# Token sums of squares: GpSimd takes the sixteenth tile too, TensorE sums one tensor instead of two, one third of a tile later

## The reference

```python
gu = jnp.einsum('bsd,hd->bsh', x, wq_gu)
gate, up = jnp.split(gu, 2, axis=-1)
h = jax.nn.silu(gate) * up
hn = rms_norm(h)            # h * rsqrt(mean(h*h over the 2048 hidden values) + eps)
return jnp.einsum('bsh,dh->bsd', hn, wq_p)
```

## Time and profile before

| | |
|---|---|
| median of three runs | 1183.12 us (1183.0 to 1185.53) |
| the profiled execution, its own time | 1185.58 us |
| its span in the trace | 1184.0 us |
| mean granted TensorE clock | 0.937 |
| TensorE busy | 1077.5 us, 91% |
| VectorE busy | 869.1 us, 73% |
| ScalarE busy | 525.2 us, 44% |
| GpSimd busy | 171.3 us, 14% |
| GpSimd's additions of squares (L2258), 52 | 79.6 us, 1532 ns each |

### The profile page before, as it was taken

How to read it: one execution, slowest core, us unless ns; L and a number is a source line. 1 busy time by engine, 2 the same in 40 slices (tenths; PEclk the granted TensorE clock), 3 DMA queues, 4 the chain that set the end, 5 groups by cost and what they waited for, 6 DMA issues and landing times. The chain is left out here.

```text
span 1184.0 us, 12999 instructions
## 1 busy us (share of the span) xinstructions
PE 1077.5 (91%) x4360; PEld 522.0 (44%) x4360; DVE 869.1 (73%) x1602; ACT 525.2 (44%) x1103; POOL 171.3 (14%) x143
## 2 busy tenths in 40 slices
PE   6788778799979999888998999999998999999997
PEld 2435545444534444334443454444444444444443
DVE  3887776756756778797687899577887677785654
ACT  3655654445525385244263364164444263531421
POOL 3100000211202221030121131122102000100100
PEclk9888765699998999899998999999999999999999
DMA  8511111532400333222130003012010011010000
GB/s 272 180 54 36 54 36 27 187 107 72 126 0 19 118 92 104 69 79 89 56 95 18 27 27 98 16 40 101 27 63 10 1 60 30 18 72 0 1 36 35
DMA packets 47618, 75.53 MB, mean 64 GB/s; under 512 B 8416, under 2 KB 16096, under 8 KB 47424
## 3 DMA queue, kind: packets, MB, share of 16 engines
q1 hardware_dynamic: 47264, 74.62, 19.9%
q0 software_dynamic: 288, 0.09, 0.2%
HBM read 66.16 MB, written 8.54 MB: 63 GB/s over the span
## 5 line engine op out<-in xcount | busy, mean ns | idle before, releaser
L1517 PE MATMUL g_g<-h,wt 128*128 128x512 f16 x1728 | 401.2, 381 | 5.8 <-DVE hid L1824 3.1
L1517 PEld LDWEIGHTS g_g<-h,wt 128*128 128x128 bf16 (+1 forms) x1728 | 168.4, 98 | 223.8 <-issue 35.5
L1531 PE MATMUL g_d<-wt,parts 128*128 128x512 bf16 (+1 forms) x864 | 208.5, 384 | 4.5 <-DVE tmp L1654 2.7
L2144 ACT ACTIVATE parts<-hid 128x512 f16<-128x512 f32 x108 | 68.0, 629 | 303.3 <-DVE hid L1824 303.2
L1439 PE MATMUL g_o<-shared 128*128 128x512 f32 x384 | 183.3, 621 | 14.4 <-DVE tmp L1613 6.4
L1817 DVE SCALAR_TENSOR_TENSOR hid<-th,g_g 128x512 f32<-128x512 f32 x108 | 73.6, 681 | 135.8 <-ACT th L2137 135.7
L1531 PEld LDWEIGHTS g_d<-wt,parts 128*128 128x128 f16 x864 | 84.1, 99 | 114.5 <-issue 16.6
L2258 POOL TENSOR_TENSOR acc<-acc,sqh 128x512 f32<-128x512 f32 x52 | 79.6, 1532 | 297.1 <-ACT sqh L2150 297.1
L1439 PEld LDWEIGHTS g_o<-shared 128*128 128x128 f32 x384 | 75.0, 199 | 98.4 <-issue 72.5
L1829 DVE TENSOR_TENSOR parts<-hid,parts 128x512 f16<-128x512 f32 x108 | 89.6, 830 | 26.0 <-ACT parts L2144 25.9
L2238 POOL TENSOR_TENSOR g_rstd<-g_var,g_power 128x4 f32<-128x4 f32 x20 | 24.2, 1210 | 328.9 <-DVE g_var L1557 328.9
(11 more groups left out here) (329 smaller groups left out, 1511.5 us busy)
## 6 DMA issues: line engine op xcount, KB each, us to landing
shared<-in_w SPq DMA_DIRECT2D x48, 256.0 KB, 2.7
x<-in_codes SPq DMA_DIRECT2D x32, 264.0 KB, 3.1
w_raw<-in_wt SPq DMA_DIRECT2D x16, 512.0 KB, 3.5
x<-in_wmod SPq DMA_DIRECT2D x7, 1024.0 KB, 5.2
wmod<-in_wmod SPq DMA_DIRECT2D x5, 1024.0 KB, 11.5
codes_f<-x SPq DMA_DIRECT2D x32, 132.0 KB, 1.7
gates<-in_x SPq DMA_DIRECT2D x4, 1024.0 KB, 8.2
shared<-in_wt SPq DMA_DIRECT2D x8, 512.0 KB, 4.7
```

The lines of the kernel that those rows point to most:

```text
L1517: mm = nc.tensor.matmul(pg[i][:], wide[:, k, o:o + P], h16[f % 2][:, s, k], start=(s == 0 and k == 0), stop=(s == 1 and k == KD - 1))
L1531: mm = nc.tensor.matmul(pd[j][:], parts16[:, t % 3, s, j * P:(j + 1) * P], wd[:, m, :], start=(m == 0 and s == 0), stop=(done and s == 1))
L2144: nc.scalar.activation(parts16[:, t % 3, 0], hid[:, t % 2], ACT.Copy).then_inc(hi_ready, 1)
```

## The change

GpSimd also adds the square of tile 15, so there are 15 additions per group. TensorE makes the token sums from `acc` alone, with four matmuls per group. The sums, their mean and their root move by one slot: on TensorE from before the group's last product to after it, on VectorE from before `low_part` to after it, right in front of `residual` (in the slot's own order the root comes before the attention steps of that slot). ScalarE's squares of a new group's first two tiles wait for GpSimd's additions, and no longer for TensorE's sums.

```diff
-    ADDS = M0 - 2
+    ADDS = M0 - 1
...
-    SUMS = [3 * M0 * (i + 1) + 1 for i in range(NG)]
+    SUMS = [3 * M0 * (i + 1) + 2 for i in range(NG)]
...
             pe.wait_ge(acc_ready, (f + 1) * ADDS)
-            pe.wait_ge(sq_ready, (f + 1) * M0)
             for j in range(NJ):
-                for i, rows in enumerate((acc, sqh[:, (M0 - 1) % 2])):
-                    mm = nc.tensor.matmul(dst[:, j:j + 1], rows[:, j * P:(j + 1) * P], ones[:, 0:1],
-                                          start=(i == 0), stop=(i == 1))
+                mm = nc.tensor.matmul(dst[:, j:j + 1], acc[:, j * P:(j + 1) * P], ones[:, 0:1], start=True, stop=True)
             mm.then_inc(full, 1)
...
                 elif f:
-                    wait_full(act, "sums", f - 1)
+                    act.wait_ge(acc_ready, f * ADDS - 1 + m)
...
-            if t < NG * M0 and 1 <= t % M0 < M0 - 1:
+            if t < NG * M0 and t % M0:
                 squares(t)
```

## The result

The changed kernel took 1187.15 us in the median of 20 runs (1183.73 to 1190.08), the kernel before 1183.21 us in the median of 20 (1179.17 to 1187.52). The ratio is 1.0028, with a 95% interval of 1.0017 to 1.0038: slower by 2.0 to 4.5 us. The forecast was 1184.7 us with a range of 1181.5 to 1187.0 and "no change" as the likeliest sign. It started from a median of 1183.12 us, and 1183.12 x 1.0028 = 1186.4 us lies inside the range. But it is slower by over 0.2%, and the interval of 2.0 to 4.5 us leaves out the +1.55 us of the forecast's own case.

What follows compares the result with a forecast made beforehand. The bound was taken to change by place: TensorE or a chain of VectorE and ScalarE. Group ends 1 to 4 gave 0.5 - 0.8 - 0.35 + 2.2 = +1.55 us on 1183.12, so 1184.7 us, range 1181.5 to 1187.0.

Steps and rivals of the forecast that it cites:

- the forecast's own case: Whole kernel: the four group ends sum to +1.55 us, giving 1184.7 us; chance 0.42.
- Group 2: End of group 2: VectorE's wait of 0.78 us for the sums goes away, -0.8 us.
- group 4: End of group 4: later root without cover and a low part held up by GpSimd's addition, +2.2 us.
- bare root: End of group 4: nothing hides the root in its new place, so VectorE waits for it, 1.25 us.
- clash: Groups 3 and 4: VectorE's low part must wait for GpSimd's fifteenth addition, about 1.0 us each.
- the end of the first launch: End of group 1: the root ends later than root and product did before, delaying TensorE's restart, +0.5 us.
- Rival 1: Every group end: TensorE is the bound, so all 3.4 us are gained, 1179.7 us; chance 0.12.
- Rivals 3 and 4: Addition holds up nothing at groups 3 and 4, 1183.3 us, chance 0.14; group 4's delay is absorbed, 1182.5 us, chance 0.08.
- group 3: End of group 3: VectorE 0.8 us late, TensorE 0.85 early; spare time at 721.70 and 729.66 leaves -0.35 us.
- TensorE's idle time before 891.46: Behind group 4: grows from 3.16 us to 4 to 5 us with VectorE's delay; otherwise the forecast is wrong.
- TensorE's 0.35 us: Group 4: TensorE gains 0.85 us, its product waits 1.2 us for the low part, leaving it 0.35 us behind.
- Rival 2: Behind group 4, at 891.46: longer TensorE idleness brings a slower clock, 1.6 us on top, 1186.3 us; chance 0.24.

Runs made afterwards that it cites:

- four matmuls alone: Kernel before with four instead of eight sum matmuls per group, leaving out the sixteenth tile's square: 1179.17 us, ratio 0.9959.
- the addition alone: Kernel before with a fifteenth GpSimd addition, eight matmuls kept, so the sixteenth tile's square counts twice: 1183.09 us, ratio 0.9995.
- old slot: Changed kernel with sums and root moved back to their earlier place in all groups: 1182.76 us, ratio 0.9985 against the kernel before.
- group 4 back: Changed kernel with only group 4's sums moved back to their earlier place: 1186.87 us, ratio 1.0022 against the kernel before.
- late slot only: Kernel before with its sums one slot later, still fourteen additions and eight matmuls: 1191.11 us, ratio 1.0053.

## Why the prediction was right or wrong

**Right, and shown: where the change acts.** Group 2 was forecast at -0.8 and gave -0.84; group 4 at +2.2 and gave +2.25, in the two parts that were named (bare root 1.25 and 1.3, clash 1.0 and 0.9); the end of the first launch at +0.5 for the restart and gave +0.37. The low parts took 1.69 and 1.77 us where 1.6 to 1.8 were forecast, the wait for the root was 1.24 us, and the product waited 1.18 us for its low part (1.2 forecast). Rival 1 (3.4 us won) was wrong by group 4, where four matmuls alone gave 0.16 us. Rivals 3 and 4 are refuted by the same rows. (In the working for group 2, 1.93 us of cover less 1.71 us leave 0.2 us and not 0.3; the root was in time all the same.)

**Wrong: group 3.** The step "At 721.70 VectorE had 0.84 us to spare, so it is just on time" failed. Forecast -0.35, measured +0.15. The bracket named ScalarE's tanh, and I took it for TensorE's time behind it; but ScalarE was itself held up by four activations that wait for VectorE. The idle time moved along with VectorE's delay. Only the idle time at 729.66 was spare: there VectorE's delay went from 0.57 to 0.17 us. It had been forecast at 0.8 us up to that place, so part of the miss is hidden: with 0.8 us and no slack at 721.70 the working would have given about +0.5.

**Wrong: what TensorE's idle time before 891.46 tells.** It grew from 3.16 to 3.95 us (4 to 5 were forecast), and the prediction calls this a sign of VectorE's delay. It is none by itself. Four matmuls alone, with VectorE 0.16 us early at group 4, gave 3.90 us, and the addition alone, with VectorE 0.93 us late, gave 3.19 us:

```profile
889.28 5.40 PE L1437 MATMUL g_o<-shared 128*128 128x512 f32 x8 [3.90 <-ACT hf L2035]
```

```profile
891.56 3.70 PE L1439 MATMUL g_o<-shared 128*128 128x512 f32 x8 [3.19 <-ACT hf L2037]
```

The idle time is VectorE's delay less TensorE's own. The term that was too small is TensorE's 0.35 us: in the changed kernel VectorE's delay reached TensorE already at 869.77 (0.40 us of waiting), and its last transposes before the projection came 1.42 us later than in the kernel before, less the 0.31 us that all engines had from earlier stages.

**Wrong: the clock's place.** The step "it ends at 396.08 ... The launch can end 0.5 us later. +0.5" counted only time and asked nothing about the clock. Rival 2 had a clock term of 1.6 us, but before 893 us, where the half-clock stretch in fact stayed at 3.4 us and cost 0.2. At the join it cost 1.5 us. That rival 2's total of 1186.3 us lies beside the measured 1186.4 us is therefore luck. Shown: the kernels with the product last, and 2.39 us of idleness or less behind it, ran on at full clock; those with one-column sums behind the product and then idleness ran on at half clock; six wide matmuls behind the sums cured it, six narrow ones didn't. By idle time alone the forecast could not have been made right, since 1.33 us with narrow matmuls was worse than 2.39 us without.

**The sum.** Without any clock the four places give 0.37 - 0.84 + 0.15 + 2.25 = +1.93 us, against +1.55 forecast. The clock adds 1.5 at the join and takes 1.4 back near 485 us; with the small rest the two profiles give +2.37 and +2.33 us, and the ratio of 20 runs says +3.3 (2.0 to 4.5). The sum was right in sign and too small. Two terms of the clock that were not in it, +1.5 and -1.4, happened to cancel; that the time still lies in the range is in part luck. "No change" was the likeliest sign, and "slower" had 0.32. The 2.4 us of the stages lie inside the interval of the runs, so nothing shows a further cost.

**Open.** The half-clock stretch near 485 us goes with the delay from the join, in all fourteen profiles, while TensorE's idle time before it is 3.15 us in all of them. Why the clock falls or comes back at just those places of the program was not settled, and no run changed the delay there and nothing else. The stretch before 891 us is as open: 3.4 us in most profiles, 6.8 us with the old slot, with group 4 back and with the late slot only, none with the addition only. Whether the clash at group 4 can be moved under a reciprocal, so that all four groups have the four matmuls, was not tried.

## What to carry to other kernels

A cheap instruction at a late place costs more than a dear one at an early place: four matmuls less won 0.7 to 1.0 us at three of four places and 0.16 us at the fourth, and a root that lost its cover took 1.3 us. Before work is handed to GpSimd, look at which two-input instruction VectorE starts within the next microsecond. A gain or loss of a microsecond also moves all later work against the changes of clock, which took or gave up to 1.7 us here. And an idle bracket is spare time only if the engine it names was not itself waiting for the idle one.

## What was not expected of the hardware

One-column matmuls did not keep TensorE's clock up: with 1.48 us of them and 1.33 us of idleness it fell from 2.4 to 1.2 GHz, and with six of 512 columns in their place (1.46 us, 1.37 us of idleness) it stayed. Equal idle times of 3.15 to 3.28 us were followed by half-clock stretches of 6.8 us, 3.4 us, or, before 891 us in the run with the addition only, by none. An execution's head, the same code in all of them, differed by up to 5.8 us between profiles (-3.64 to +2.12), which is more than anything the change did. Yet less this delay the first half-clock stretch behind the head's end begins at the same places in all of them: 396.0 to 396.1 us at the join in the five that have it there, 484.8 to 484.9 us in the other nine.
